# Attention and feed-forward with experts on one core: one narrow run a group, long rows masked on VectorE, loads reordered

## The reference

```python
x = x + layernorm(attention(layernorm(x)))
x = x + layernorm(ffn(layernorm(x)))
```

```python
scores = q @ k.T / sqrt(32); scores = where(causal, scores, -1e20)
out = softmax(scores) @ v @ w_o.T + b_o
result = x @ base_w.T + base_b + 2.0 * sum_e gate_e * (x @ A_e.T) @ B_e.T
```

## Time and profile before

| | |
|---|---|
| median of 3 runs | 1130.16 us (1129.71 to 1131.78) |
| profiled execution | 1130.88 us |
| its span | 1128.9 us |
| busy: TensorE, VectorE, ScalarE, GpSimd | 95%, 54%, 36%, 36% |
| mean granted TensorE clock | 0.983 |

### The profile page before, as it was taken

How to read it: one execution, slowest core, us unless ns; L and a number is a source line. 1 busy time by engine, 2 the same in 40 slices (tenths; PEclk the granted TensorE clock), 3 DMA queues, 4 the chain that set the end, 5 groups by cost and what they waited for, 6 DMA issues and landing times.

```text
span 1128.9 us, 17668 instructions
## 1 busy us (share of the span) xinstructions
PE 1077.6 (95%) x6944; PEld 867.1 (77%) x6944; DVE 612.4 (54%) x1244; ACT 404.4 (36%) x674; POOL 410.4 (36%) x461
## 2 busy tenths in 40 slices
PE   4989999999999999999999995899999999999995
PEld 3879898898866666666666653799999999999995
DVE  7454433434465655556556532766556666656654
ACT  7032322201056666665665662322222222222221
POOL 1072543324346656566665552111111121211210
PEclk8989999999999999999999997899999999999999
DMA  9052331264255665435344425323222222232200
GB/s 361 21 186 94 134 142 71 102 159 124 98 176 149 172 181 141 118 102 149 101 121 111 113 81 170 91 89 90 83 75 75 75 75 75 75 95 92 76 19 37
DMA packets 77489, 127.04 MB, mean 113 GB/s; under 512 B 7648, under 2 KB 46944, under 8 KB 74336
## 3 DMA queue, kind: packets, MB, share of 16 engines
q1 hardware_dynamic: 77408, 125.93, 36.8%
HBM read 85.01 MB, written 40.37 MB: 111 GB/s over the span
## 4 chain that ended last, share of the span: by engine, by line
PE 92%; DVE 2%; DMA 2%; ACT 1%; POOL 1%; issue 1%; SPq 0%; POOLq 0%; DVEq 0%; ACTq 0%
PE bank L1197 19%; PE bank L1199 19%; PE bank L1198 19%; PE bank L1293 9%; PE bank L1307 7%; PE bank L1270 7%; PE bank L1324 4%; PE bank L1273 3%; PE bank L1405 1%; PE bank L1206 1%; DMA q_t<-shift_l 1%; DMA den_i<-inv_scratch 1%; DVE ln_st L898 0%; DVE turn L935 0%; DMA x<-x 0%
## 5 line engine op out<-in xcount | busy, mean ns | idle before, releaser
L954 DVE TENSOR_REDUCE neg_max<-bank 128x1 f32<-128x384 f32 (+3 forms) x352 | 213.8, 637 | 165.6 <-PE bank L1273 165.4
L789 ACT ACTIVATE prob<-bank 128x512 f32<-128x512 f32 x320 | 184.0, 600 | 113.5 <-PE bank L1293 113.5
L618 POOL TENSOR_TENSOR ln_rs<-ln_ve,minus_half 128x1 f32<-128x1 f32 x64 | 62.7, 980 | 420.8 <-DVE ln_mm L903 420.8
L1293 PE MATMUL bank<-q_t,k_t 98*128 98x512 f32 x320 | 145.0, 471 | 1.9 <-DMA q_t<-shift_l 0.9
L1270 PE MATMUL bank<-k_t,q_t 96*128 96x384 f32 (+3 forms) x512 | 136.9, 324 | 0.0
L1197 PE MATMUL bank<-xt_h,wq_h 128*128 128x512 f32 x320 | 128.5, 402 | 5.4 <-DVE xt_l L915 5.4
L659 POOL TENSOR_SCALAR_AFFINE_SELECT prob<-prob 128x512 f32<-128x512 f32 x128 | 82.5, 646 | 135.5 <-ACT prob L789 135.4
L1197 PE MATMUL bank<-wf_h,xt_h 128*128 128x384 f32 (+1 forms) x384 | 129.8, 338 | 1.8 <-DVE z L1108 1.8
L1199 PE MATMUL bank<-wf_l,xt_h 128*128 128x384 f32 (+1 forms) x384 | 130.2, 339 | 0.0
L1198 PE MATMUL bank<-wf_h,xt_l 128*128 128x384 f32 (+1 forms) x384 | 130.0, 339 | 0.0
L1198 PE MATMUL bank<-xt_h,wq_l 128*128 128x512 f32 x320 | 126.4, 395 | 0.0
(11 more groups left out here) (105 smaller groups left out, 1888.0 us busy)
## 6 DMA issues: line engine op xcount, KB each, us to landing
q_t<-q_scratch SPq DMA_DIRECT2D x32, 512.0 KB, 5.1
q_scratch<-turn_h SPq DMA_DIRECT2D x16, 512.0 KB, 2.7
q_scratch<-turn SPq DMA_DIRECT2D x16, 512.0 KB, 2.9
q_t<-q_scratch SPq DMA_DIRECT2D x32, 256.0 KB, 5.3
att_scratch<-att SPq DMA_DIRECT2D x32, 256.0 KB, 2.0
at_raw<-att_scratch SPq DMA_DIRECT2D x16, 512.0 KB, 3.7
x<-x SPq DMA_DIRECT2D x16, 512.0 KB, 4.3
den_i<-inv_scratch SPq DMA_DIRECT2D x60, 128.0 KB, 4.9
```

The lines of the kernel that those rows point to most:

```text
L618: nc.gpsimd.tensor_tensor(ln_rs[j][:], ln_ve[j][:], minus_half[:], ALU.pow).then_inc(count, 1)
L789: nc.scalar.activation(prob[n % 2][:, i, :, :].rearrange("p h q -> p (h q)"), bank[3 + (NS * n + i) % 3][:], ACT.Exp, scale=INV_SQRT_HD).t ...
L954: nc.vector.tensor_reduce(neg_max[n % 2][:, heads[0]:heads[-1] + 1, qb], row_bank(n, i)[:, 0:len(heads) * w].rearrange("p (h k) -> p h k", ...
L1293: mm(bank[3 + (NS * n + i) % 3][:].rearrange("p (h q) -> p h q", q=P), k_t[s][0:KROWS + 2, P * kc:P * kc + P], q_t[s][0:KROWS + 2, :, P * ...
```

## The change

- In `order` the four V and D come in one run between R3 and S4; S and R alternate otherwise.
- For groups from 2 on the one-head tiles R3 to R10 lose the mask product. VectorE adds a mask from SBUF (`row_mask`, 128 x 512, zeros and the causal block at its end, loaded once) and takes the maximum in one call, which writes the masked scores back into the bank.
- Maxima are kept with their sign; the two copies behind T negate.
- The projection weights come in two halves of 768 columns, all first halves first; their splits stand behind those of tiles 0 to 3. Tile 4 is split behind pair 1, not pair 2.
- The second output tile gets a buffer of its own for the denominators (`den_second`) and is loaded in step 30, scaled in step 31; its split moves ahead on both engines. x's first tile is loaded ahead of the last weights. `att` and `den_sb` change places, so that it waits for less.

```diff
-        return {2: TT, 3: TT + 1, 4: TT + 2}.get(p)
+        return {1: TT, 3: TT + 1, 4: TT + 2}.get(p)
...
+        row_mask = Map(m.at)("row_mask", [P, SEQ])
...
+        att = [m("att0", [P, SEQ])]
+        m = Map(x1_at + D * 4, D * 4)
+        att.append(m("att1", [P, SEQ]))
         den_sb = m("den_sb", [P, SEQ])
...
+        den_second = Map(m.at)("den_second", [P, KC, P])
...
+        def masked_later(n, i):
+            return n >= 2 and len(ROWS[i][1]) == 1
...
-            def load_wq(c):
-                sp.dma_start(wq_raw[:, c, :], w_qkv[:, c, :]).then_inc(wq_loaded[c], 16)
+            def load_wq(c, j):
+                cols = slice(WQ_FIRST * j, WQ_FIRST if j == 0 else QKV)
+                sp.dma_start(wq_raw[:, c, cols], w_qkv[:, c, cols]).then_inc(wq_loaded[j][c], 16)
...
+            sp.wait_ge(proj_ps, PROJECTED)
+            sp.dma_start(row_mask[:], row_mask_h).then_inc(mask_loaded, 16)
             load_v(0)
...
                 if t == 0:
-                    sp.wait_ge(den_stored, 16 * NG)
                     sp.wait_ge(att_stored[0], 16 * (NG // 2))
                 elif t == 1:
-                    for j in range(2):
-                        sp.wait_ge(att_stored[j], 16 * (NG // 2))
+                    sp.wait_ge(den_stored, 16 * NG)
+                    sp.wait_ge(att_stored[1], 16 * (NG // 2))
...
                 if n == NG - 2:
+                    load_att(1)
+                    load_inverses(1)
                     sp.wait_ge(score_ps, NS * (NG - 1))
                     load_ffn(1)
+            load_res(0)
...
             load_ffn(7)
-            load_att(1)
-            load_inverses(1)
             store_att(NG - 1)
             store_den(NG - 1)
-            load_res(0)
             load_res(1)
...
-            wq_to_hi(0)
             transposed1(2)
             transposed1(3)
-            for c in range(1, KC):
-                wq_to_hi(c)
+            for j in range(2):
+                for c in range(KC):
+                    wq_to_hi(c, j)
...
-                nc.scalar.copy(shift_h[n % 2][:], shift_bank(n)[0:REP * TT, 0:P]).then_inc(shift_hi, 1)
+                nc.scalar.activation(shift_h[n % 2][:], shift_bank(n)[0:REP * TT, 0:P], ACT.Copy, scale=-1.0
+                                     ).then_inc(shift_hi, 1)
...
+            split_att(1)
+            normalise_y(0)
             split_ffn(2)
-            split_att(1)
             copy_values(NG - 1)
             copy_sums(NG - 1)
-            normalise_y(0)
...
+                scored = row_bank(n, i)[:, 0:len(heads) * w]
+                if masked_later(n, i):
+                    if n == 2:
+                        dve.wait_ge(mask_loaded, 16)
+                    nc.vector.tensor_tensor_reduce(
+                        out=scored, in0=scored, in1=row_mask[:, SEQ - w:SEQ], scale=1.0, scalar=LOWEST,
+                        op0=ALU.add, op1=ALU.max, accum_out=row_top[n % 2][:, heads[0], qb:qb + 1]).then_inc(row_max, 1)
+                else:
...
                 if n == NG - 1:
                     split_ffn(1)
+                    scale_att(1)
                     project_bias(0, 1)
                     y_statistics(0)
+            split_att(1)
             split_ffn(2)
-            scale_att(1)
-            split_att(1)
             residual1(0)
             split_ffn(3)
             split_ffn(4)
+            project_bias(1, 0)
+            lo2(0)
             split_ffn(5)
             split_ffn(6)
-            project_bias(1, 0)
-            lo2(0)
...
+                if masked_later(n, i):
+                    last.then_inc(row_ps, 1)
+                    return
...
+            pe.wait_ge(wq_ready, 2 * KC)
             project_pair(0, 3)
...
-            order = ("S0 R0 R1 V0 S1 R2 T S2 R3 V1 S3 R4 R5 V2 S4 R6 V3 S5 R7 S6 R8 D "
-                     "S7 R9 S8 R10 S9").split()
+            order = ("S0 R0 S1 R1 S2 R2 T S3 R3 V0 V1 V2 V3 D S4 R4 R5 "
+                     "S5 R6 S6 R7 R8 S7 R9 S8 R10 S9").split()
```

More of the change, by code:

```diff
@@ L158, in build @@
         bias_v = m("bias_v", [P, VD])
-        neg_max = [m(f"neg_max{j}", [P, REP, TT]) for j in range(2)]
+        row_top = [m(f"row_top{j}", [P, REP, TT]) for j in range(2)]
         shift_h = [m(f"shift_h{j}", [REP * TT, P], F32R) for j in range(2)]
@@ L218, in build @@
         m = Map(m.at + SPILL, cd_size + SPILL)
+        row_mask = Map(m.at)("row_mask", [P, SEQ])
         y = m("y", [P, D])
         x1_at = m.at
+        att = [m("att0", [P, SEQ])]
+        m = Map(x1_at + D * 4, D * 4)
+        att.append(m("att1", [P, SEQ]))
         den_sb = m("den_sb", [P, SEQ])
-        att = [m(f"att{j}", [P, SEQ]) for j in range(2)]
         m = Map(f_at, f_size)
@@ L272, in build @@
         k_ones = sem("k_ones")
-        wq_loaded = [sem(f"wq_loaded{c}") for c in range(KC)]
+        wq_loaded = [[sem(f"wq_loaded{c}_{j}") for c in range(KC)] for j in range(2)]
         wq_hi = sem("wq_hi")
@@ L399, in _ @@
             load_first(3)
-            for c in range(KC):
-                load_wq(c)
+            for j in range(2):
+                for c in range(KC):
+                    load_wq(c, j)
             sp.dma_start(causal[:], causal_h).then_inc(causal_loaded, 16)
@@ L724, in transposed1, with wq_to_hi @@
                 last.then_inc(xt_hi, 1)
-            def wq_to_hi(c):
-                act.wait_ge(wq_loaded[c], 16)
-                nc.scalar.copy(wq_h[:, c, :], wq_raw[:, c, :]).then_inc(wq_hi, 1)
+            def wq_to_hi(c, j):
+                cols = slice(WQ_FIRST * j, WQ_FIRST if j == 0 else QKV)
+                act.wait_ge(wq_loaded[j][c], 16)
+                nc.scalar.copy(wq_h[:, c, cols], wq_raw[:, c, cols]).then_inc(wq_hi, 1)
             def rope_to_hi(b, p):
@@ L953, in maxima @@
                     wait(dve, shift_ps, n - 1)
-                nc.vector.tensor_reduce(neg_max[n % 2][:, heads[0]:heads[-1] + 1, qb],
-                                        row_bank(n, i)[:, 0:len(heads) * w].rearrange("p (h k) -> p h k", k=w),
-                                        AX_X, ALU.max, negate=True).then_inc(row_max, 1)
+                scored = row_bank(n, i)[:, 0:len(heads) * w]
[6 more added lines that the diff above has]
+                else:
+                    nc.vector.tensor_reduce(row_top[n % 2][:, heads[0]:heads[-1] + 1, qb],
+                                            scored.rearrange("p (h k) -> p h k", k=w), AX_X, ALU.max
+                                            ).then_inc(row_max, 1)
             def shift_lo(n):
                 dve.wait_ge(shift_hi, n + 1)
-                nc.vector.tensor_tensor(shift_l[n % 2][:], shift_bank(n)[0:REP * TT, 0:P],
-                                        shift_h[n % 2][:].bitcast(F32), ALU.subtract).then_inc(shift_sb, 1)
+                nc.vector.scalar_tensor_tensor(out=shift_l[n % 2][:], in0=shift_bank(n)[0:REP * TT, 0:P], scalar=-1.0,
+                                               in1=shift_h[n % 2][:].bitcast(F32), op0=ALU.mult, op1=ALU.subtract
+                                               ).then_inc(shift_sb, 1)
             for t in range(TT):
                 stats1(t)
-            lo1(0)
-            lo1(1)
-            wq_to_lo(0)
-            lo1(2)
-            lo1(3)
-            for c in range(1, KC):
-                wq_to_lo(c)
+            for t in range(TT):
+                lo1(t)
+            for j in range(2):
+                for c in range(KC):
+                    wq_to_lo(c, j)
             dve.wait_ge(ident_loaded, 16)
@@ L1269, in row_scores @@
                 for at, h in enumerate(heads):
-                    mm(dst[:, w * at:w * at + w], q_t[s][0:KROWS, h, P * qb:P * qb + P], k_t[s][0:KROWS, 0:w],
-                       start=(at == 0), stop=False, skip_group_check=True)
+                    last = mm(dst[:, w * at:w * at + w], q_t[s][0:KROWS, h, P * qb:P * qb + P], k_t[s][0:KROWS, 0:w],
+                              start=(at == 0), stop=masked_later(n, i), skip_group_check=True)
+                if masked_later(n, i):
+                    last.then_inc(row_ps, 1)
+                    return
                 diagonal = dst[:, 0:len(heads) * w].rearrange("p (h k) -> p h k", k=w)[:, :, P * qb:w]
@@ L1488, in table @@
         return np.ascontiguousarray(np.repeat(t.T, P // (HD // 2), axis=0))
+    causal = np.where(np.tril(np.ones((P, P), bool)), 0.0, MASKED).astype(np.float32)
     inputs = {
@@ L1501 @@
         "ident": np.eye(P, dtype=np.float32),
-        "causal": np.where(np.tril(np.ones((P, P), bool)), 0.0, MASKED).astype(np.float32),
+        "causal": causal,
+        "row_mask": np.concatenate([np.zeros((P, SEQ - P), np.float32), causal], 1),
         "before": np.tril(np.ones((EXP, EXP), np.float32), -1)[None],
```

24 lines of the change are left out of this document (16 added, 8 removed).

## The result

| | before | after |
|---|---|---|
| median | 1129.93 us (1128.59 to 1131.78) | 1098.22 us (1096.71 to 1099.09) |
| span of the profiled execution | 1128.9 | 1097.1 |
| VectorE, ScalarE, GpSimd busy | 54%, 36%, 36% | 56%, 36%, 38% |

A forecast was written before the change was run, and what follows sets the result against it. TensorE, busy 95% of the span, was taken to bound the kernel, with VectorE pacing the changed loop. Loop 19.4, start 5.3 and seam 15.0 sum to 39.7 us off 1130.88, so 1091 us, range 1076 to 1117.

The forecast's parts named there:

- Step: 6.14 + 1.80 + 2.92 = 10.86 us, VectorE's: Attention loop: VectorE's chain of maxima paces a step, 6.14 + 3x + 4y, at 10.86 us instead of 11.53.
- x and y: Attention loop: start-to-start cost of VectorE's add-and-maximum, 0.60 us for a 384 tile (x), 0.73 for 512 (y).
- rival (a): Attention loop: the add-and-maximum costs no more than a plain maximum, ScalarE paces, 1079 us in all; chance 0.17.
- ScalarE's bound lies just under: Attention loop: ScalarE's chain would need 10.5 us a step, and 10.1 in the last 5 steps, under VectorE's 10.86.
- the pair at 0.73: Attention loop, a sign: VectorE's pass and its one-column read together take 0.73 us from start to start.
- over 2 us a step: Attention loop: TensorE's own saving from fewer mask products and a single run of values and denominators, over 2 us a step.
- The loop, 19.4 forecast: Attention loop: 29 full steps, each going from 11.53 to 10.86 us, gain 19.4 us.
- I take 1.6: Start: tiles 5 and 6 split later than their slack cost 1.6 us, from between nothing and 3.7.
- The seam, 15.0 forecast: Between attention loop and feed-forward: feed-forward starts at 707.9 instead of 722.9 us, gain 15.0 us.
- (b): Attention loop: pass and read are serial, 11.98 us a step, 1124 us in all, half way 1107; chance with half way 0.11.
- (c): Attention loop: VectorE's pass takes each element twice as long, a step of 14.2 us, 1188 in all; chance 0.10.
- (d): Seam: it doesn't close, SP blocked or splits ahead of the residual; loop and start alone give 1106 us; chance 0.07.

The follow-up runs named there:

- e4: The changed kernel with ScalarE's copy of the values and its output-weight piece put ahead of S4's exp, into the narrow run; 1085.28 us.
- e5: e4 with ScalarE's copy of the sums also moved ahead of S4's exp; 1082.88 us.
- e3: The changed kernel with a plain maximum in place of the add-and-maximum, the long rows' mask left out; 1097.89 us.
- e1: The changed kernel with TensorE's order of before, five interleaved runs of values and denominators a step; 1101.03 us.
- e12: e10 with S3 moved from ahead of the run to behind R3, and ScalarE's three instructions ahead of exp 3 instead of exp 4; 1072.17 us.
- e10: e6 with e8's edit, the two bias rows loaded in steps 12 and 13, the first residual ahead of VectorE's third weight split; 1075.51 us.
- e6: e5 with the run of values ahead of R3 on TensorE; 1081.55 us.
- e2: The changed kernel with the long tiles' mask products back on TensorE and plain maxima on VectorE; 1099.82 us.
- e9: The changed kernel with the seam's loads and the ScalarE and VectorE orders behind the loop as before the change; 1110.96 us.
- e8: The changed kernel with tiles 5 and 6 handed in one pair of heads earlier; 1094.49 us.

## Why the prediction was right, and where it was not

The direction, the size (1098 for 1091, range 1076 to 1117) and the three places were right. The engine that sets the loop was not, and one of the four sums was half of what was said.

**The step, 10.86 forecast, 10.85 measured, by two errors that cancel.** "Step: 6.14 + 1.80 + 2.92 = 10.86 us, VectorE's" fails in x and y. I took 0.60 and 0.73 by adding the read to a pass of 0.66; measured are 0.515 and 0.65. With these the same formula gives 6.14 + 1.55 + 2.60 = 10.29, and e4 and e5, where ScalarE is out of the way and VectorE paces, ran at 10.34: the formula holds, the prices did not. With the reciprocal's 0.86 it gives 11.15, and in the change itself those steps take 11.13. That is rival (a), whose price was nearly right (a plain maximum has 0.60 and 0.49) and whose time (1079) was not, because it rested on the other failed step, "ScalarE's bound lies just under". Its first part, 4.2 us to S0, is right (4.13). The second, S0 to S3 with R0 to R2 and T "2.1 us, then 0.5", is 2.91 from S0 to V0: 2.54 up to R3 (507.10 to 509.64) and 0.37 for R3. That makes 10.85 in all, not 10.5 (and the four terms as written already add up to 10.57). e3 and e4 show it from both sides: cheaper maxima give nothing, ScalarE's copies elsewhere give 13 us. The last steps, which have no weight piece on ScalarE, agree: 10.43 to 10.57 instead of 10.85. So the wrong engine was named, and that the step came out to 0.01 us is luck. Of the signs that I gave, the step of 10.9 came; the pair at 0.73 did not (0.65), nor a VectorE that is never idle between R4 and R1 (0.36 ahead of R0), and TensorE waits for an exp at S0 (0.32), which I had tied to a step of 10.5 or less.

**What TensorE saves.** Masks: 0.9 to 1.2 us a step forecast, 0.51 measured (e1), 0.064 each. The 0.15 ahead of the narrow run was the dearest of eleven, and "about 0.11" for the others was too much. The single run: 0.5 to 1.1 forecast. e1 to e12, with the same instructions, is 11.02 - 10.19 = 0.83, and e12 still has waits, so the upper half or more. Of "over 2 us a step" 1.34 is shown; how much more the waits of e12 hide stays open. It decided nothing, since another engine paced.

**The loop, 19.4 forecast, 16.0 measured.** Steps 1 to 29 gained 17.2 (324.28 to 307.06), where 28 steps of 0.67 make 18.8. The largest loss is step 9, 14.41 us instead of 12.73 before. TensorE and SP's queue, after:

```profile
418.56 0.50 PE L1326 MATMUL bank<-q_t,k_t 98*128 98x512 f32 x1 [2.42 <-DMA q_t<-shift_l]
```

```profile
406.40 0.34 SPq L579 DMA_DIRECT2D bo_row<-b_o  x1
406.80 0.42 SPq L580 DMA_DIRECT2D bf_row<-b_ffn  x1
...
409.53 0.73 SPq L479 DMA_DIRECT2D q_t<-shift_h  x1
410.30 0.59 SPq L479 DMA_DIRECT2D q_t<-shift_l  x1
```

The shift rows stand behind two broadcast loads and a group's loads. e10 moved the two and the stall went. That a shorter step leaves the rows less time is my reading and not shown. With the two loads in place, step 9 takes 11.45 us (e6) to 16.30 (e2) in the traces, so a difference of 1 or 2 us between medians above can come from there. I had asked what each moved load waits for, and not which loads lose slack when every step gets shorter. Three steps with the reciprocal (11.13 instead of 10.85) cost 0.9 in all. Another term, the -1.53 us at the very end, is the clock of the last rows above, not the change. At the ends of the loop, steps 30 and 31 have waits of 2.5 us in sum (V3 for GpSimd 0.74, scores for exps), where before had 0.43.

**The start.** The split weights gave at least what was said: the first product starts at 20.31 us, before 21.00, and tile 4's transposes at 54.84, before 56.12, 1.28 us where 0.5 was forecast. Tile 4's stall went with its low clock, as forecast (3.7 and 2.7). The failed term is "I take 1.6" for the later tiles: they wait 0.61 and 2.43, and from 80 to 100 us the clock is 0.91, 1.8 us. That makes 4.8, so that of 6.4 only 1.6 was left (54.24 to 52.64 us, tile 4 to tile 8). The upper end that I gave, "the 3.7 us that went", left out that a stall that returns can bring the low clock with it; in e2, e6 and e9 the same waits did not. e8 shows that 5.5 of the 6.4 were to be had (54.24 to 48.73).

**The seam, 15.0 forecast, 14.5 measured**, and 13.4 in e9. The split ahead of the residual (1.28 us from 672.17 to 673.45, forecast 1.3) and the low clock behind the 5.49 us wait (0.69 from 680 to 690) came as written; the transposes and the second half took 9.2 us (8.5 forecast). The first half's products end at 675, and TensorE waits again, for the chain that was named.

**The other rivals.** (b) and (c) asked for a dear pass. The pass over 512 columns takes 0.73 us, and its read begins together with the next pass. The Trainium skill, Perfetto Trace Analysis, § Optimizing Scalar/DVE Operations, says that half of an instruction's profiled overhead overlaps with the next one. That a part of it does shows here: 0.73 for the pass beside 0.65 from start to start. The halving of rival (c) did not occur with one source in a bank. The rule of the Trainium skill that the prediction names beside (c) speaks of two sources in SBUF, and nothing here is against it. (d), an open seam, did not come. No run here has the operation with both sources in SBUF, so the halving itself stays untested.

## What to carry to other kernels

Before you add up what a change saves on the busiest engine, write for each other engine the chain from the event that starves it to the event that it frees, with the instructions that happen to stand between; here a copy and a cast of 0.5 us each, in the wrong place, cost 13 us. Gathering one engine's work into a run starves the others for as long: give them what they have that needs nothing new (copies, casts) just then. And when every step gets shorter, look at the loads with the least slack and at what follows a stall, not only at the stall.
